# Interleaving the second half of an attention with the first half's router: a two-group transformer block on one core

## What is computed

```python
h = token_layer(ids, mask, rel_dist, ...)              # (4, 512, 64)
x = layernorm(h)
# attention: phases by tanh and sin/cos, cumulative sums over the positions
combined = mh_out + kv_ret
lnx = (combined - mu) / sqrt(var + 1e-5) * ln_g + ln_b
h = h + (x + lnx @ out_w + out_b)
x2 = layernorm(h)
idx = top_k(x2 @ Wg + bg, 2)                           # 2 of 8 experts
y = sum over chosen e of gelu(x2 @ W1[e] + b1[e]) @ W2[e] + b2[e]
out = h + y
```

## Time and profile before

| | |
|---|---|
| runs | 190.92, 196.98, 197.11 us; median 196.98 us |
| profiled execution | 191.07 us, of which its span (first to last instruction) 189.4 us |
| busy in the span | PE 138.8, DVE 127.1, ACT 77.2, POOL 31.6 us |
| mean granted TensorE clock | 0.836 of full speed |
| last-ending chain | PE 43%, DVE 36%, DMA 7%, issue 5%, ACT 4% |

### The profile page before, as it was taken

How to read it: one execution, slowest core, us unless ns; L and a number is a source line. 1 busy time by engine, 2 the same in 40 slices (tenths; PEclk the granted TensorE clock), 3 DMA queues, 4 the chain that set the end, 5 groups by cost and what they waited for, 6 DMA issues and landing times.

```text
span 189.4 us, 2093 instructions
## 1 busy us (share of the span) xinstructions
PE 138.8 (73%) x682; PEld 83.5 (44%) x682; DVE 127.1 (67%) x343; ACT 77.2 (41%) x126; POOL 31.6 (17%) x52
## 2 busy tenths in 40 slices
PE   0699959599960494699597233529999799979991
PEld 0382625227750212658486222526766355444430
DVE  6957895789499698999868899983330887012011
ACT  2010251436366431885752022335514365545541
POOL 3022210407105342342400232010000000000000
PEclk9999996957997558559969755585899999999999
DMA  5799934000000000000000000000000000002011
GB/s 142 268 394 362 398 134 114 0 0 0 0 0 0 0 0 0 3 2 2 0 0 3 2 0 0 0 0 2 0 3 0 0 0 3 0 0 55 0 28 28
DMA packets 7138, 9.20 MB, mean 49 GB/s; under 512 B 2388, under 2 KB 4436, under 8 KB 7128
## 3 DMA queue, kind: packets, MB, share of 16 engines
q1 hardware_dynamic: 7128, 9.07, 14.3%
HBM read 8.55 MB, written 0.52 MB: 48 GB/s over the span
## 4 chain that ended last, share of the span: by engine, by line
PE 43%; DVE 36%; DMA 7%; issue 5%; ACT 4%; SPq 3%; POOL 1%; DVEq 0%; ACTq 0%
PE bank L907 8%; DMA dist_sb<-in_dist 7%; PE bank L891 5%; PE bank L892 3%; PE bank L689 3%; DVE rs_a L957 2%; PE bank L778 2%; PE bank L704 2%; PE bank L662 2%; DVE st_sum L969 1%; PE bank L701 1%; PE bank L697 1%; PE bank L706 1%; DVE rs_v L966 1%; DVE dist_sb L1000 1%
## 5 line engine op out<-in xcount | busy, mean ns | idle before, releaser
L582 ACT ACTIVATE hid<-bank 128x512 f32<-128x512 f32 x32 | 18.0, 599 | 21.4 <-PE bank L892 21.3
L1284 DVE TENSOR_TENSOR h<-bank,h 128x256 f32<-128x256 f32 x4 | 1.7, 422 | 23.2 <-PE bank L917 23.2
L907 PE MATMUL bank<-hid,ffn_sb 128*64 128x512 f32 x64 | 16.8, 614 | 0.0
L891 PE MATMUL bank<-xp,w1hi 128*128 128x512 f32 x32 | 15.1, 473 | 0.4 <-ACT xp L566 0.4
L1198 DVE TENSOR_TENSOR dist_sb<-bank,early_sb 128x256 f32<-128x256 f32 x16 | 6.0, 419 | 10.3 <-PE bank L783 9.5
L892 PE MATMUL bank<-xp,w1lo 128*128 128x512 f32 x32 | 12.9, 402 | 0.0
L1000 DVE TENSOR_TENSOR dist_sb<-dist_sb,mask_in 128x1024 f32<-128x1024 f32 x8 | 9.4, 1220 | 4.3 <-POOL mask_in L331 4.3
L639 PE MATMUL bank<-dist_sb,neigh 128*64 128x512 f32 x32 | 10.3, 713 | 0.0
L891 PEld LDWEIGHTS bank<-xp,w1hi 128*128 128x128 f32 x32 | 6.3, 195 | 8.7 <-ACT hid L582 5.2
L674 PE MATMUL bank<-early_sb,x 128*128 128x128 f32 x8 | 1.7, 352 | 9.1 <-DVE gsum L1099 8.5
L778 PE MATMUL bank<-dist_sb 64*128 64x256 f32 x16 | 6.7, 506 | 2.2 <-DVE dist_sb L1198 2.0
(11 more groups left out here) (249 smaller groups left out, 352.9 us busy)
## 6 DMA issues: line engine op xcount, KB each, us to landing
dist_sb<-in_dist SPq DMA_DIRECT2D x4, 1024.0 KB, 10.9
mask_in<-in_mask SPq DMA_DIRECT2D x4, 256.0 KB, 10.1
ffn_sb<-in_ffn SPq DMA_DIRECT2D x1, 816.0 KB, 10.9
fold_sb<-in_folded SPq DMA_DIRECT2D x1, 772.0 KB, 12.4
late_sb<-in_late SPq DMA_DIRECT2D x1, 728.5 KB, 11.5
mask_in<-in_mrows SPq DMA_DIRECT2D x1, 512.0 KB, 3.6
out<-h SPq DMA_DIRECT2D x8, 64.0 KB, 1.7
early_sb<-in_early SPq DMA_DIRECT2D x1, 391.0 KB, 3.1
```

Source lines behind the costliest of these rows:

```text
L582: nc.scalar.activation(hid[:, at % HB], bank[hid_bank[at % 3]][:, :], ACT.Gelu).then_inc(S["hid_set"], 1)
L891: nc.tensor.matmul(o, w1hi[:, e * HID:(e + 1) * HID], xp1[g][:, toks], start=True, stop=False)
L907: mm = nc.tensor.matmul(bank[2][j * D:(j + 1) * D, :], K["e_w2"][:, (e + j) * D:(e + j + 1) * D], hid[:, (at + j) % HB], start=False, stop ...
```

## The change

The table `ORDER` is rewritten from the last third of group 0's chunks on. Group 1's remaining `queries` slots now stand before group 0's residual and `experts` slots, and group 1's chunks before any `hidden` product; the slots of group 0's `experts` up to the router and its top two lie between group 1's chunks. On PE `chunks(1)` no longer waits for `h3_set` and `var_read`: group 0's output product goes to bank 2 and its variance to bank 1 (`attn_bank`, `var_bank`). Some slots are split by added `yield`s (the top two on DVE after the first choice, the scaling of `x2` from its reciprocal root), and ACT's second `copy_y` stands at step 18, one slot earlier.

```diff
-ORDER = ("T0 T0 T0 T1 T0 T1 ...
-         "P1 C0 Q1 C0 Q1 C0 C0 Q1 C0 C0 Q1 C0 C0 X0 Q1 X0 Q1 X0 C1 Q1 X0 X0 Q1 C1 X0 C1 X0 C1 X0 C1 X0 C1 X0 "
+         "Q1 C0 Q1 C0 C0 Q1 C0 C0 Q1 C1 Q1 Q1 C0 Q1 Q1 C1 C0 X0 C1 X0 C1 X0 C1 X0 X0 C1 X0 C1 X0 C1 X0 X0 C1 X0 X1 "
...
+        attn_bank = (2, 5)
+        var_bank = (1, 4)
...
                     if n == 10:
                         copy_y(0)
+                    if n == 18:
+                        copy_y(1)
...
-                copy_y(1)
                 yield
...
             def chunks(g):
                 pe.wait_ge(S["k_feat"], 2 * g + 2)
                 pe.wait_ge(S["kang_set"], 8)
-                if g == 0:
+                if g:
+                    pe.wait_ge(S["s_masked"], 2 * NC * g)
+                else:
                     pe.wait_ge(S["h_set"], NG)
-                pe.wait_ge(S["h3_set"], g) if g else pe.wait_ge(S["h1_copied"], NG)
-                if g:
-                    pe.wait_ge(S["var_read"], g)
+                    pe.wait_ge(S["h1_copied"], NG)
...
                 pe.wait_ge(S["comb_sq"], g + 1)
+                if g == 0:
+                    pe.wait_ge(S["st_set"], NG)
+                    pe.wait_ge(S["center_set"], 2 * NG)
                 for c in range(NC):
-                    mm = nc.tensor.matmul(bank[4][:, c * NH_:(c + 1) * NH_], sq_c[:, c * P:(c + 1) * P], K["half_ones"],
+                    mm = nc.tensor.matmul(bank[var_bank[g]][:, c * NH_:(c + 1) * NH_], sq_c[:, c * P:(c + 1) * P], K["half_ones"],
...
-                    mm = nc.tensor.matmul(bank[5][:, c * P:(c + 1) * P], cc_t[:, c * P:(c + 1) * P], outw_g[:, :],
+                    mm = nc.tensor.matmul(bank[attn_bank[g]][:, c * P:(c + 1) * P], cc_t[:, c * P:(c + 1) * P], outw_g[:, :],
...
                 rsqrt(st_r[:, :], 8)
+                yield
                 dve.wait_ge(S["x2t_mm"], g + 1)
...
                     if k == 0:
                         link(nc.vector.scalar_tensor_tensor(out=score[:], in0=sel[:], scalar=-3.0e38, in1=score[:],
                                                             op0=ALU.mult, op1=ALU.add))
+                        yield
```

More of the change, by code:

```diff
@@ L78 @@
        ("tie", P, E)]
-ORDER = ("T0 T0 T0 T1 T0 T1 T0 T0 T1 T0 T1 P0 P0 T1 P0 T1 Q0 P0 T1 W0 P0 Q0 P1 Q0 Q0 P1 Q0 Q0 Q0 Q0 P1 C0 P1 "
-         "P1 C0 Q1 C0 Q1 C0 C0 Q1 C0 C0 Q1 C0 C0 X0 Q1 X0 Q1 X0 C1 Q1 X0 X0 Q1 C1 X0 C1 X0 C1 X0 C1 X0 C1 X0 "
-         "C1 X0 C1 X0 C1 X0 X0 X1 X0 X0 X1 X0 X0 X0 X1 X0 X0 X0 X1 X0 X0 X1 X1 X1 X1 X1 X0 X1 X1 X1 X1 X1 X1 "
-         "X1 X1 X1 X1 X1 X1 X1 X1 X1 X1").split()
+ORDER = ("T0 T0 T0 T1 T0 T1 T0 T0 T1 T0 T1 P0 P0 T1 P0 T1 Q0 P0 T1 W0 P0 Q0 P1 Q0 Q0 P1 Q0 Q0 Q0 Q0 P1 C0 P1 P1 C0 "
+         "Q1 C0 Q1 C0 C0 Q1 C0 C0 Q1 C1 Q1 Q1 C0 Q1 Q1 C1 C0 X0 C1 X0 C1 X0 C1 X0 X0 C1 X0 C1 X0 C1 X0 X0 C1 X0 X1 "
+         "X0 X0 X1 X0 X0 X1 X0 X0 X1 X0 X0 X1 X0 X0 X1 X0 X0 X1 X0 X0 X0 X0 X1 X1 X1 X1 X1 X0 X1 X1 X1 X1 X1 X1 X1 "
+         "X1 X1 X1 X1 X1 X1 X1 X1").split()
 def follow(stages):
@@ L408, in experts @@
             def experts(g):
-                for _ in range(25):
+                for _ in range(27):
                     yield
@@ L1221, in chunks @@
                 dve.wait_ge(S["var_mm"], g + 1)
-                nc.vector.tensor_scalar(rs_v[:, 0:8], bank[4][:, 0:8], EPS, None, ALU.add).then_inc(S["var_read"], 1)
+                nc.vector.tensor_scalar(rs_v[:, 0:8], bank[var_bank[g]][:, 0:8], EPS, None, ALU.add).then_inc(S["var_read"], 1)
                 dve.wait_ge(S["var_read"], g + 1)
@@ L1226, in chunks @@
                 dve.wait_ge(S["attn_mm"], g + 1)
-                link(nc.vector.tensor_tensor(v8(comb[:]), b3(5), bc(st_c[:, :], D), ALU.mult))
+                link(nc.vector.tensor_tensor(v8(comb[:]), b3(attn_bank[g]), bc(st_c[:, :], D), ALU.mult))
                 dve.wait_ge(S["hx_set"], g + 1)
```

## The result

| | before | changed |
|---|---|---|
| median of 22 runs each, us | 192.72 (190.15 to 197.11) | 195.44 (191.21 to 198.6) |
| ratio of undisturbed runs | | 1.0073 [1.0038, 1.0107] |
| profiled execution, us | 191.07 | 198.38, span 196.7 |
| busy PE / DVE in the span, us | 138.8 / 127.1 | 145.0 / 127.3 |
| mean granted TensorE clock | 0.836 | 0.787 |

The changed kernel is slower, by 0.7% with an interval that excludes no change; the forecast was 1.45 us (0.75%) faster. It is within 2%, as forecast, but its sign is wrong. That its median of 195.44 lies beside the predicted 195.5 is luck: the forecast had carried its difference to 196.98, the median of three runs, and over 22 runs before has 192.72. The ratio leaves out the longer executions of each kernel (13 of the changed kernel's 22 took over 194 us, and 4 of before's 22), which the medians, 1.4% apart, hold.

What follows compares the result with a forecast made beforehand. VectorE was taken as the bound from 107.0 to 129.7 us, TensorE after it. -8.3 + 6.9 - 1.65 + 1.6 = -1.45 us, carried to the median 196.98, gave 195.5 us, range 188.0 to 199.0.

Steps and rivals of the forecast that it cites:

- step 2: From group 1's query features through its chunks: its centred residual comes at 143.0 instead of 151.26, gain 8.3 us.
- step 5: TensorE idles some 2.3 us before group 1's centring ends; the low clock after it costs 1.6 us (bounds 0, 3.2).
- Step 3: At 143.0 TensorE still has six `hidden`, three `back` and one bias product to do: 6.9 us lost again.
- Step 4: At the seam of the groups TensorE's waits of 0.44 us (`xp2` copies) and 1.21 (`copy_y`) vanish: 1.65 us.
- Step 1: On VectorE, group 1's query features end at 119.0 instead of 129.68: 12.16 us moved behind, 1.5 us of stalls stay.
- The clock holds: The 2.3 us gap before group 1's `x2` transposes is not punished: -3.05 us, 193.9 on the median; chance 0.16.
- the whole lead is kept: TensorE is not the bound after 143 and the 8.3 us stay: 188.7 on the median; chance 0.04.
- the slower rival: TensorE at 1.2 GHz through the chunks (3.5 us), low stretch twice as long (1.6): +3.7, 200.7; chance 0.12.
- The level of the runs: Difference carried to the median of three listed times, 196.98; a rival at the shorter level, 189.6, had chance 0.26.

Runs made afterwards that it cites:

- warm_chunks: The changed kernel with 21 extra unread TensorE products in the idle time before group 1's query-feature transposes; ratio to before 1.0030.
- before_copy: The kernel before with one edit, group 0's second `copy_y` one slot earlier, at step 18; ratio to before 0.9887.
- fill_work: The changed kernel with two of group 0's `experts` slots moved ahead of group 1's `x2` transposes; ratio to before 0.9837, in a second run 0.9758.
- warm_chunks2: The changed kernel with 11 extra unread TensorE products before group 1's query-feature transposes; ratio to before 0.9890.
- warm_gap2: The changed kernel with two extra unread TensorE products in the idle time before group 1's `x2` transposes; ratio to before 0.9883.

## Why the prediction was wrong, step by step

The forecast was -1.45 us on the stage; it is +1.39. The difference of 2.84 is 1.7 in step 2 and 1.35 in step 5, less 0.2 in steps 3 and 4. So step 2 failed, which took the clock to be up in the chunks, and in step 5 the price of the low stretch was too small. With either of the two as forecast, the stage would be near 0 instead of 1.39 longer.

- **Step 1 was right.** The features end 12.56 us after `mag`, against 12.5. The two POOL stalls moved as assumed: `L967`, eight columns wide, took 0.98 us at 119.45 (0.17 elsewhere) and `L957` 1.15 at 117.38 (0.43 in its other half), while POOL's two products with `mag` ran from 119.36 and from 117.17. Together they are 1.53 us, against 1.5. By the rule of the Trainium skill that the forecast named ("SBUF — State Buffer", section "SBUF: two separate sides") a VectorE instruction with two SBUF inputs waits for the POOL instruction, and the trace agrees for `L967`. `L957` has one SBUF input, so what the forecast took from that section doesn't cover it, and it was stalled all the same.
- **Step 2 failed in one term, the clock of the chunks.** First masking at 17.68 (17.7 forecast), the `xp2` transposes and variance 1.97 (2.1) and the last chain 4.88 (4.88) were right. But "the chunk steps of TensorE and its `xp1` transposes lie under this if the clock is up", and it was not: 0.50 over 130.0 to 139.6. VectorE waited 0.56 and 1.60 us, and the centring came at 38.15 instead of 36.5. warm_chunks shows that the clock costs 2.24 us there; at full clock the stretch would have been 0.6 us shorter than forecast. The gain of the stretch is 6.60 us instead of 8.3.
- **The argument behind it was the weak point.** I argued that TensorE is "nearly always busy", as it was before 134 us where the clock came back. It was nearly always busy here too (9.00 of 9.60 us), and the clock stayed down for 15 us after 125.02. Why it stayed down so long is not shown. In the kernel before, 512-column `hidden` products lay among the chunks and the clock was back at 134.0, 6.7 us after TensorE's work began at 127.34 (with one wait of 0.43); the change takes just these products away, which makes them a suspect. But no run puts them back among the chunks, and elsewhere in the same trace the clock came back at 123.7 behind 128-column transposes alone. These are stretches of the kernel before, over those transposes, the idle time behind them and the first products among the chunks:

```profile
120.30:123.60 3.30, 3.29 (x16) 3.27 (x16) 3.20 (x7) 2.25 (x5) 0.93 (x1) 0.50 0.00 0
123.90:127.00 3.10, 0.01 (x1) 0.00 (x0) 2.69 (x13) 0.63 (x2) 0.00 (x0) 1.00 0.00 0
...
129.80:133.80 4.00, 4.00 (x17) 3.13 (x17) 0.05 (x1) 2.75 (x5) 0.00 (x0) 0.50 0.01 2
```

And this is the changed kernel in its chunks, without a wait of TensorE and still low:

```profile
131.30:139.90 8.60, 8.60 (x59) 7.45 (x57) 6.99 (x27) 0.33 (x1) 0.00 (x0) 0.50 0.00 1
```

The Trainium skill's "TensorE: Matmul & The Clock Gate", section "HAM oscillation — how this bites in real kernels", speaks against bursts with waits between them. The low clock in the chunks is what the forecast made of that rule, and it gave it too little (0.12). The trace agrees in part: the clock was lost in the 13.51 us idle time. But it doesn't show that waits between the bursts kept it lost: it stayed low over 8.6 us without a wait, and in warm_chunks the same bursts, busy 12.36 of 15.40 us, kept 1.00.

- **Step 3 was right.** Held at full clock, what TensorE has left after the transposes is 39.6 us against 34.57: 5.04 more. The forecast has 6.9 for the backlog less 1.65 for the stalls, 5.25.
- **Step 4 was right.** The rows at 172.84 and 174.91 have no wait before them, and before_copy shows 1.21 and 0.44 to be separate. Nothing is late in their place.
- **Step 5 had the mechanism and half the size.** The idle time was 2.57 us (2.3 forecast). The price is 42.56 - 39.61 = 2.95 us, not 1.6; its upper bound, 3.2, held. The step had taken the price from one case, in which the idle time was 1.96 us and the low stretch 3.2 us long. Here it came in both sizes: 3.3 us once, 6.7 and 6.8 in two other kernels.
- **The rivals.** "The clock holds" and "the whole lead is kept" are out. The truth lies between the forecast and the slower rival. The long low stretch of that rival came in full; its chunk price of 3.5 us came at half, 1.7, since most of the slow pieces are covered by VectorE's own work. Its sign, a centring "later than about 144.5", was met: carried to before's time of `mag`, the centring ended at 150.56 - 5.9 = 144.66. But the tipping point itself lay earlier. With the 7.99 us that the part behind the centring really lost (42.56 - 34.57), the change breaks even with a centring at 151.26 - 7.99 = 143.3, just behind the forecast's 143.0.
- **The level of the runs** was a guess from three executions, and 22 of them moved before's median by 4.3 us. Of the 7.3 us between the two profiled spans 5.9 lie ahead of `mag`, where the new order has changed nothing on VectorE. Whether the changed kernel has such long executions more often than before stays open.

## What to carry to other kernels

When a reordering makes one engine's hand-over earlier, price the idle time it opens on the other engine twice: once as lost work and once as the clock it may lose, and put real work into it before anything else. Here two table entries (fill_work) turned a loss of 0.7% into a gain of some 2%. And read the granted clock over the work that now stands behind a longer idle time, not only TensorE's busy time: here the chunks lay behind 13.51 us of idle time instead of among long products, TensorE looked busy, and they ran at half clock until 140 us.

## What the runs showed of the hardware

- **Busy time didn't tell the clock.** The same chunk instructions ran at 1.00 in warm_chunks with TensorE busy 12.36 of 15.40 us, and at 0.50 in warm_chunks2 with it busy 9.40 of 9.40. What differed was what ran before: 17.0 of 17.0 us of long products, against 9.38 of 12.0 (112 to 124 us) and then 2.57 of 5.4 until the clock fell. Which of these two decided is not shown. A longer busy time at low clock is partly the low clock itself: eight transposes take 1.97 us there and 1.09 at full clock.
- **The same idle time had different prices.** After 2.57 us the low stretch was 6.7 us (changed) and 3.3 (warm_chunks2); after 2.58 in warm_chunks it began only some 1.2 us after the work resumed and lasted 6.8. After 0.86 us (warm_gap2) and 1.37 us (before, ahead of 151.31) none followed.
